# New places for every stage of a software-pipelined layer kernel, and expert gathers in packs of four

## The reference, cut to what matters

```python
x = x + mamba(layernorm(x))      # conv, selective scan with 16 states over 256 channels, a feed-forward net
x = x + experts(layernorm(x))    # first expert block
x = x + ssm(layernorm(x))        # a scan with 16 gated states, projections, tanh, layernorm
x = x + experts(layernorm(x))    # second expert block, same weights
```

## Time and profile before

| | us |
|---|---|
| median of 3 runs | 2137.09 (2133.57 to 2138.39) |
| the profiled execution, first to last instruction | 2189.7 |
| of it: first gating to last gating (15 intervals) | 127.3 to 1908.8 |
| behind the last gating (the drain) | 280.9 |
| PE / DVE / ACT / POOL busy | 1681.9 / 1767.2 / 1543.5 / 1355.7 |

### The profile page before, as it was taken

One profiled execution on the slowest core, in us unless ns is written; L12 is line 12 of the kernel. 1 busy time (PEld: TensorE's weight loads), 2 busy tenths in 40 slices (PEclk: granted clock), 3 DMA queues, 4 the chain that ended last, 5 costly groups with the idle time before them and its releaser, 6 DMA issues. The chain is left out here.

```text
span 2189.7 us, 24718 instructions
## 1 busy us (share of the span) xinstructions
PE 1681.9 (77%) x6097; PEld 937.5 (43%) x6186; DVE 1767.2 (81%) x4204; ACT 1543.5 (70%) x3276; POOL 1355.7 (62%) x1209
## 2 busy tenths in 40 slices
PE   4887878787887978888888879788878877754562
PEld 2332435354544545454544444454544444433342
DVE  3898989798988989898898989898889997733331
ACT  4565868587877868787878778777877765554542
POOL 0226463667776667677676676677677776566554
PEclk8898989998999999998999989999989988886776
DMA  2001120222222222222222222322222222233222
GB/s 54 0 10 56 32 65 23 62 66 75 82 80 77 70 84 68 82 77 65 84 80 77 73 84 68 84 68 74 76 75 82 72 80 73 71 87 92 78 82 71
DMA packets 79901, 151.06 MB, mean 69 GB/s; under 512 B 20584, under 2 KB 46592, under 8 KB 79680
## 3 DMA queue, kind: packets, MB, share of 16 engines
q0 software_dynamic: 49152, 134.28, 21.3%
q1 hardware_dynamic: 29344, 14.65, 2.4%
q10 hardware_dynamic: 1248, 0.34, 0.1%
HBM read 145.01 MB, written 4.19 MB: 68 GB/s over the span
## 5 line engine op out<-in xcount | busy, mean ns | idle before, releaser
L1466 POOL DMA_INDIRECT rows<-in_experts,index x1024 | 980.8, 958 | 477.6 <-issue 363.2
L1352 DVE TENSOR_TENSOR_SCAN hp<-dA,fed_ps 128x1024 f32<-128x1024 f32 x256 | 582.3, 2275 | 7.0 <-issue 5.8
L783 PE MATMUL ysum<-hp,ident 128*128 128x512 f32 x1024 | 503.9, 637 | 16.0 <-DVE hp L1362 9.0
L1481 POOL TENSOR_TENSOR hp<-hp,c_row 128x1024 f32<-128x1024 f32 x112 | 263.9, 2356 | 279.2 <-ACT c_row L1043 179.8
L1336 DVE TENSOR_TENSOR fed_ps<-du,b_ps 128x1024 f32<-128x1024 f32 x256 | 313.4, 1224 | 58.4 <-remote 26.3
L1026 ACT ACTIVATE dA<-delta,decay 128x511 f32<-128x511 f32 x512 | 334.8, 711 | 15.8 <-issue 7.9
L1005 ACT ACTIVATE rows<-rows,coef 128x128 f32<-128x128 f32 x1024 | 311.0, 390 | 19.2 <-DVE coef L1272 19.2
L783 PEld LDWEIGHTS ysum<-hp,ident 128*128 128x128 f32 x1024 | 215.0, 211 | 251.3 <-issue 218.5
L1265 DVE CUSTOM_DVE_ANT_0 rows<-rows,xn 128x128 f32<-128x128 f32 x1024 | 261.5, 318 | 51.7 <-DMA rows<-in_experts,index 51.2
L933 ACT ACT_TABLE_LOAD x218 | 279.7, 1283 | 8.8 <-PEq L543 5.0
L716 PE MATMUL bank<-rows,ident 128*128 128x256 f32 x1024 | 247.4, 397 | 34.0 <-ACT rows L1005 33.4
(11 more groups left out here) (182 smaller groups left out, 2357.6 us busy)
## 6 DMA issues: line engine op xcount, KB each, us to landing
rows<-in_experts,index POOLq DMA_INDIRECT x1024
x_in<-in_x SPq DMA_DIRECT2D x16, 256.0 KB
x_res<-in_x SPq DMA_DIRECT2D x16, 256.0 KB
y<-x SPq DMA_DIRECT2D x16, 256.0 KB
rows<-in_taps SPq DMA_DIRECT2D x1, 512.0 KB
rows<-in_wq_t SPq DMA_DIRECT2D x1, 512.0 KB, 5.3
rows<-in_in_proj_t ACTq DMA_DIRECT2D x1, 256.0 KB
rows<-in_key_t SPq DMA_DIRECT2D x1, 128.0 KB, 5.2
```

The source lines that it names most:

```text
L783: mm = nc.tensor.matmul(ysum[:, j, :], ident[:], hp[:, BUFFER[k], j, :], start=(k == SUM_ORDER[0]), stop=(k == SUM_ORDER[-1]))
L1352: nc.vector.tensor_tensor_scan(flat, dA[:, n % NDA, :, :].rearrange("p a b -> p (a b)"), fed_ps[:].rearrange("p a b -> p (a b)"), 0.0, ALU ...
L1466: pool.indirect_dma_start(e.rows[:, t, h, :], None, A["experts"], bass.IndirectOffsetOnAxis(ap=e.index[:, t, h:h + 1], axis=0)).then_inc(e ...
L1481: pool.tensor_tensor(state, state, c_row[:, k % NCR, :].unsqueeze(1).to_broadcast([P, NH, T]), ALU.mult).then_inc(pool_read, 1)
```

## The change

Nothing is computed differently and no transfer is added or dropped. Two things change.

First, the gathers. A pack is one part, 4 gathers. Each of the 8 packs of a batch has its own semaphore. Pack p waits for pack p - 2, the last but one, where before a tile waited for the whole of the tile before. At most 8 gathers of a block are under way, as before. `dot` waits for its first pack and, after four heads, for the second.

Second, nearly all entries of the two tables move. The code of it, and the lines of the tables that are spoken of below:

```diff
-    "dve_square_x": (PRE, (6,)),
+    "dve_square_x": (PRE, (2,)),
-    "dve_shift_x": (PRE, (8,)),
+    "dve_shift_x": (PRE, (4,)),
-    "dve_weigh_e1": (POST, (72, 85)),
+    "dve_weigh_e1": (POST, (66, 82)),
-    "dve_weigh_e2": (POST, (227, 243)),
+    "dve_weigh_e2": (POST, (224, 239)),
-    "act_norm_b": (POST, (113,)),
+    "act_norm_b": (POST, (120,)),
-    "dve_index_e2": (POST, (181, 196)),
+    "dve_index_e2": (POST, (183, 198)),
-    "dve_top_e2": (POST, (178, 180, 182, 184)),
+    "dve_top_e2": (POST, (177, 180, 184, 185)),
-    "pool_fetch_e1": (POST, (43, 43, 47, 47, 61, 61, 61, 62)),
-    "pool_fetch_e2": (POST, (201, 202, 208, 217, 217, 217, 227, 228)),
+    "pool_fetch_e1": (POST, (39, 42, 44, 53, 61, 62, 66, 70)),
+    "pool_fetch_e2": (POST, (192, 201, 205, 209, 214, 219, 223, 228)),
...
-    "pool_fetch_e1": (POST, (43, 43, 47, 48, 61, 61, 61, 62)),
-    "pool_fetch_e2": (POST, (196, 196, 205, 205, 214, 215, 224, 224)),
+    "pool_fetch_e1": (POST, (35, 37, 47, 47, 48, 49, 53, 62)),
+    "pool_fetch_e2": (POST, (176, 177, 204, 210, 212, 219, 220, 227)),
...
@@ -401,7 +402,7 @@
                 self.picks = sem(f"e{n}_picks")
                 self.indexed = sem(f"e{n}_indexed")
                 self.opened = sem(f"e{n}_opened")
-                self.fetched = [sem(f"e{n}_fetched{t}") for t in range(NT)]
+                self.fetched = [sem(f"e{n}_fetched{p}") for p in range(2 * NT)]
                 self.dotted = sem(f"e{n}_dotted")
                 self.gelu = sem(f"e{n}_gelu")
                 self.weighed = sem(f"e{n}_weighed")
@@ -1259,8 +1260,9 @@
                                         ALU.add).then_inc(e.indexed, 1)
 
             def experts_dot(e, r, n, t):
-                dve.wait_ge(e.fetched[t], (n + 1) * (16 * HEADS))
                 for h in range(HEADS):
+                    if h % PACK == 0:
+                        dve.wait_ge(e.fetched[2 * t + h // PACK], (n + 1) * (16 * PACK))
                     row = e.rows[:, t, h, 0:P]
                     op = nc.vector.tensor_tensor_reduce(row, row, e.xn[r][:, t, :], 1.0, 0.0, ALU.mult, ALU.add,
                                                         e.dot[:, t, h:h + 1])
@@ -1454,18 +1456,18 @@
         def _(pool):
             def fetch(e, n, part):
 
-                t, first = part // 2, part % 2 * (HEADS // 2)
-                if part % 2 == 0 and t:
-                    pool.wait_ge(e.fetched[t - 1], (n + 1) * (16 * HEADS))
+                t, first = part // 2, part % 2 * PACK
+                if part >= 2:
+                    pool.wait_ge(e.fetched[part - 2], (n + 1) * (16 * PACK))
                 if part % (2 * HALF) == 0:
                     pool.wait_ge(e.indexed, at(n, 2, t // HALF))
                     if later(n):
                         pool.wait_ge(e.summed, at(n - 1, 2, t // HALF))
                 pool.sem_inc(e.opened, 1)
-                for h in range(first, first + HEADS // 2):
+                for h in range(first, first + PACK):
                     pool.indirect_dma_start(
                         e.rows[:, t, h, :], None, A["experts"],
-                        bass.IndirectOffsetOnAxis(ap=e.index[:, t, h:h + 1], axis=0)).then_inc(e.fetched[t], 16)
+                        bass.IndirectOffsetOnAxis(ap=e.index[:, t, h:h + 1], axis=0)).then_inc(e.fetched[part], 16)
 
             def iteration(i, q, has):
                 if isinstance(i, int) and i == 0:
```

More of the change, by code:

```diff
@@ L42 @@
 HALF = NT // 2
+PACK = HEADS // 2
 LEAD = 3
@@ L69 @@
[L69 to L74, removed]
-    "pe_gate": (POST, (122,)),
[L76 to L95, removed]
+    "pe_ff1": (POST, (0,)),
+    "pe_ff2": (POST, (7,)),
+    "pe_ln_a": (POST, (10,)),
@@ new lines @@
+    "pe_sum_e2": (POST, (236, 251)),
+    "act_rstd_x": (PRE, (1,)),
+    "act_rms_x": (PRE, (3,)),
+    "act_keep_x": (PRE, (10,)),
+    "act_norm_x": (PRE, (4,)),
+    "act_turn_x": (PRE, (6,)),
+    "act_conv": (PRE, (14, 19, 24, 28)),
+    "act_silu": (PRE, (30, 63)),
+    "act_dbl": (PRE, (34,)),
+    "act_soft": (PRE, (42, 47)),
+    "act_split": (PRE, (37, 41)),
+    "act_exp": (PRE, (55,)),
+    "act_ln": (PRE, (56,)),
+    "act_out": (POST, (1,)),
+    "act_gelu": (POST, (2,)),
+    "act_rstd_a": (POST, (5,)),
@@ new lines @@
+    "pool_delta": (PRE, (59,)),
+    "pool_x1": (POST, (4,)),
+    "pool_x3": (POST, (120,)),
+    "pool_fetch_e1": (POST, (39, 42, 44, 53, 61, 62, 66, 70)),
+    "pool_fetch_e2": (POST, (192, 201, 205, 209, 214, 219, 223, 228)),
+    "sp_xres": (POST, (14,)),
+    "sp_store": (POST, (234,)),
+}
+LAST_SLOTS = {
+    "pe_out": (POST, (1,)),
+    "pe_ff1": (POST, (2,)),
+    "pe_ff2": (POST, (9,)),
+    "pe_ln_a": (POST, (11,)),
+    "pe_turn_e1": (POST, (27,)),
+    "pe_sim_e1": (POST, (27, 28, 35, 35)),
+    "pe_flip_e1": (POST, (33, 38)),
+    "pe_code_e1": (POST, (33, 43)),
+    "pe_sum_e1": (POST, (87, 89)),
+    "pe_turn_b": (POST, (106,)),
+    "pe_xp": (POST, (108,)),
+    "pe_gate": (POST, (114,)),
+    "pe_y": (POST, (120,)),
+    "pe_z": (POST, (133,)),
+    "pe_ln_c": (POST, (147,)),
+    "pe_turn_e2": (POST, (155,)),
+    "pe_sim_e2": (POST, (164, 171, 178, 180)),
+    "pe_flip_e2": (POST, (172, 187)),
+    "pe_code_e2": (POST, (173, 200)),
+    "pe_sum_e2": (POST, (240, 244)),
@@ new lines @@
+    "act_rstd_a": (POST, (8,)),
+    "act_rstd_e1": (POST, (17,)),
+    "act_norm_e1": (POST, (24,)),
+    "act_turn_e1": (POST, (26,)),
+    "act_flip_e1": (POST, (32, 42)),
+    "act_gelu_e1": (POST, (55, 74)),
+    "act_scale_e1": (POST, (57, 60, 79, 82)),
+    "act_out_e1": (POST, (87, 89)),
+    "act_rstd_b": (POST, (94,)),
+    "act_norm_b": (POST, (101,)),
+    "act_turn_b": (POST, (107,)),
+    "act_xp": (POST, (113,)),
+    "act_gate": (POST, (114,)),
+    "act_tanh": (POST, (122,)),
+    "act_rstd_c": (POST, (134,)),
```

193 lines of the change are left out of this document (79 added, 114 removed).

## The result

The changed kernel takes 1967.06 us (median of 4 runs, 1957.38 to 1988.53) against 2135.33 us before: ratio 0.9198 [0.9158, 0.9237], 168 us less. The 1988.53 was a slow run, and the ratio is that of the fast ones. A second set, `after_again`, gave 1963.18 us (median of 6), 0.9173 [0.9134, 0.9212].

A forecast was written before the change was run, and what follows sets the result against it. The prediction took VectorE's instruction list to bound the loop and GpSimd's string of gathers with holes the drain. Drain and iteration 15 gave -33, the loop -16: -49 from 2137.09, so 2088 us, range 2072 to 2104.

The forecast's parts named there:

- The packs: In the drain, GpSimd's 16 holes at tile boundaries shrink from 2.55 to 0.30 us: -37 us; nothing in the loop.
- Gathers moved ahead: 16 gathers move from the drain into iteration 15: -20 us in the drain, +4 us in iteration 15.
- The new holes: In the drain, GpSimd waits for batch 15's first indices: 16 us at e1, some 12 at e2 (+16 and +4).
- The loop: VectorE's order and waits in loop iterations: -1.6 us an iteration, ten iterations, -16 us.
- All together -2.8: Loop, VectorE's stretched small operations: coef1 -1.6, coef2 -1.2, `square_x` -1.0, `off1` +1.0 us an iteration.
- `off1`: In the loop, `off1` moved behind scan 5 and can be caught by GpSimd's product instead: +1.0 us an iteration.
- the bound of -5: Lower bound per loop iteration: the whole excess of coef and `m` goes, 4.6 us.
- a mean of `coef` near 600 ns: Sign in the profile after: VectorE's mean `coef` falls from 1147 ns to near 600.
- Rival 2: Loop gains more, all stretched small operations go: -5 an iteration over 11, -33 in the drain, 2049 us; chance 0.17.
- The waits: VectorE's loop waits, us an iteration: -0.6 at the spread of B, +0.7 for e2's transposition ahead of it, +1.1 for `gelu`.
- rival 3: Loop gets slower, VectorE waits for the index; at 5 us an iteration +22, 2159 us; chance 0.10.
- rival 4: Drain gathers get longer beside dots, 51 us over its 20 tiles: 2139 us; chance 0.04.

The follow-up runs named there:

- packs_only: Changed code with the gathers' packs but both old tables of places; 2089.69 us, ratio 0.9761 to the kernel before.
- tables_only: Old code, one semaphore for a tile, with both new tables of places; 1982.84 us, ratio 0.9267 to the kernel before.
- loop_table: Changed kernel with the new loop table but the old last table (except x3's place); 1975.53 us, ratio 0.9239 to the kernel before.
- late16_again: Changed kernel with the last table used from iteration 16 on, so iteration 15 has the loop's places; 1944.99 us, ratio 0.9114.
- before_again: The unchanged kernel before, profiled a second time; 2142.46 us, one run, with a profiled span of 2140.7 us.
- probes: Seven small VectorE products added per iteration to the changed kernel, placed where GpSimd's product still runs; 2065.41 us, ratio 0.9641 to the kernel before.
- small_forward: Packs, new last table and old loop table, with only weigh_e1, weigh_e2, square_x and shift_x at new loop places; 2146.24 us, ratio 1.0037.
- chains_back: Changed kernel with VectorE's four small entries and their neighbouring ScalarE and TensorE stages at old loop places; 2219.90 us, ratio 1.038.
- probe_apart: Changed kernel with seven small VectorE products added per iteration, placed where GpSimd's product is over; 2016.63 us, ratio 0.9423 to the kernel before.
- before_short2: Same kernel as before_short: the kernel before with seven GpSimd products an iteration cut to 8 of 512 tokens; before_short took 2025.09 us, ratio 0.9466.

## Why the prediction was wrong

**The packs: right, with the old tables.** Forecast -37 for the holes; `packs_only` shows -34 in the drain, and the holes sum to 21 us in place of 62. With the new tables in place they are worth 13 us there (`tables_only`). The reading that a pack has landed before the next but one is asked for holds: no wait at a pack of 2.5 us is left.

**Gathers moved ahead: the sum right, the path not.** 160 gathers stand behind the last product. With the old loop places and packs, the new last table takes 6 us off the drain (245.8 to 239.5 us) and adds 8 to iteration 15 (120.9 to 129.3); with the new loop places (`loop_table` to the changed kernel) both get shorter, iteration 15 from 133.0 to 125.9 and the drain from 244.8 to 239.4. The new holes were to be 16 and 12 us, both behind an index. The first index came as forecast (1755.75, 39.6 us behind the gating; forecast 41), but GpSimd reached it 36 us behind the gating and not 25, and the hole is 5 us. The other three (5.8, 7.5 and 6.3 us) end with a sum of TensorE. For the last block the prediction let the sum move behind the codes and counted only that the index comes earlier; the gather waits for the same sum. That 25 us came out where 28 were forecast is luck. Iteration 15 measured +5.6 for a forecast of +4 (+0.8 in `after_again`); that it could be 17 to 22 us shorter with the loop's places (`late16_again`) was not seen.

**The loop: here it failed.** The step is "All together -2.8" for the stretched operations; it measured -10. Three things went wrong in it. First, I took only operations whose own entry moved past a scan. A meeting depends on the order of both engines around it, so entries that stay put count as well: the first dot products behind scans 13 (2.7 us an iteration in `before_again`) and 4 (0.6) were left at nothing although had their mean of 322 ns, and it is 286 now. Second, `off1` was to be caught anew (+1.0) and is not; `off` had lost 1.0 us an iteration in the kernel before, and that went too. Third, the bound of -5 left out the dots, s and off. The groups of the trace of the kernel before held the whole sum of 9.5 us (coef 3.9, dots 2.5, m 1.4, off 1.0, s 0.7), and the bound should have been that sum. The sign that was named, a mean of `coef` near 600 ns, came out at 165. Rival 2 named the mechanism but priced it at -5.

**The waits: small, but of the wrong sign.** Forecast +1.2 an iteration, measured -1.9 of idle: 3.1 us, or 34 us over eleven iterations, is the second part of the miss. The wait ahead of `top` fell by 2.7 us an iteration, of which the prediction kept nothing, since it let a wait for the index take its place; the wait ahead of L1249 (bits, the first step of the index) fell from 0.5 to 0.2 (rival 3 had it grow). Of the +1.1 for `gelu` and `weigh` 0.1 is seen, and the wait for the spread of B, priced at +0.7, fell from 0.9 to 0.3. The 1.0 us that did come stands ahead of L1364, which no term had.

**The number of iterations.** Ten were counted, but the stretches ahead of the loop gained too: start and iterations 1 to 3 gave 25 us more, and eleven gating intervals lie in 4 to 14.

**Why such operations stand still.** The Trainium skill, SBUF — State Buffer, section "SBUF: two separate sides", says that VectorE's operations with two SBUF inputs and GpSimd's operations that read SBUF exclude each other for a whole instruction, and whoever starts first keeps the ports. The prediction used that section for gathers alone, where no row bore it out (0.96 us a gather in both kernels, rival 4); the section's warning on gathers is about VectorE's operations in a 2-port performance mode, and the dots, with two SBUF inputs, are its other case, so the prediction stretched it. For products the traces agree with the exclusion: probes and coef end with the product. They agree in the exception too: beside products in the changed kernel, 67 feed products and 68 scans, which have an operand in PSUM, took at most 0.02 us more than usual.

Two things in the traces go beyond this. By the recorded starts, 20 of the 50 stretched operations in ten iterations of `before_again` began 0.07 to 0.6 us before the product, each right behind a gather, and still stood until its end: the coef of 1084.49 above is one. So the order of the recorded starts does not tell who is held. And `index`, which reads one tensor in SBUF, took 1.13 us in place of 0.18 beside a product in `small_forward` (10 of 40), while `st`, the statistics, which also reads one, took its usual 0.28 us there (20 of 80). The section would have `index` held if it runs in a 2-port mode; whether it does, no trace shows. That it is the ports and no other shared part, no run here shows.

**What stays open.** Why just this table avoids nearly every meeting cannot be put down to single entries: each partial mix of the loop's table brought meetings or waits back. What the waits gave by themselves was not tried apart; the 1.9 us an iteration are the difference of two traces.

## What to carry to other kernels

Sum the excess of every VectorE group over its shortest form before costing a reordering: that sum, and not the part you can trace to a moved entry, is what can be won there (about 10 us of the 11.3 an iteration here; shorter waits come on top), and cutting the other engine's instruction short in one run tells whether it is real. Tables of places work as a whole: each small part that was moved alone cost more than it was worth, and so did one moved with its nearest neighbours (`chains_back`). Look at each stretch against its neighbour: an iteration with less work that lasts longer (125.9 against 107 us) was a gain of 18 us for one line.

## What the runs showed of the hardware

Adding seven operations of 0.17 us an iteration where hardly any met a product (`probe_apart`) cost 6.0 us an iteration, of which 1.2 is their own time. The granted clock was 0.91 in iterations of 119 us, and 1.00 (the 2.4 GHz level throughout) in the changed kernel's iteration from 949.5, with TensorE busy 94.2 in place of 101.5 us for the same 379 matmuls. In `before_short2` it rose from 0.91 to 0.97, and TensorE's busy time fell to 96.9 us, though nothing but the length of GpSimd's products was changed: there a higher clock came with fewer stalls of VectorE, and not from an edit of TensorE's work. VectorE's waits fell by only 1.9 us an iteration from `before_again` to the changed kernel. One execution of before_short took 5113 us with a recorded clock of 1.000, its 1024 sums L783 at 1780 ns each (652 ns in `before_again`); the other five executions of that kernel took 2021 to 2025 us. It is left out above, and I have no cause for it.
